# Last cross-attention of a four-layer Perceiver: the four query pieces of a tile spread over four steps, in banks 7, 5, 7 and 5

## The reference, cut to what matters

```python
def _L3_xattn_ref(image_embeds, latents, ln1_g, ln1_b, ln2_g, ln2_b, Wq, Wkv, Wo):
    x = layer_norm(image_embeds, ln1_g, ln1_b)          # (64, 257, 128)
    l = layer_norm(latents, ln2_g, ln2_b)               # (64, 32, 128)
    q = l @ Wq                                          # 16 heads of 64
    k, v = jnp.split(jnp.concatenate([x, l], axis=1) @ Wkv, 2, axis=-1)
    q, k, v = (to_heads(q), to_heads(k), to_heads(v))
    w = jax.nn.softmax(jnp.einsum('bhqd,bhkd->bhqk', q * scale, k * scale))
    out = jnp.einsum('bhqk,bhkd->bhqd', w, v)
    return out.transpose(0, 2, 1, 3).reshape(B, S_lat, INNER) @ Wo
x = x + _L3_xattn_ref(ctx_1024, _layernorm(x, axis=-1), ...)
```

## Time and profile before

| | us |
|---|---|
| median of 3 runs | 2186.41 (2182.8 to 2187.88) |
| profiled execution | 2167.64 |
| its span, first to last instruction | 2165.7 |
| mean granted TensorE clock | 0.916 |

### The profile page before, as it was taken

The page is one execution under the profiler, slowest core; times in us unless marked ns, Lnnn a source line. Parts: engine busy times, 40 slices in busy tenths (PEclk is TensorE's granted clock), DMA queues, the critical chain, the costliest instruction groups (busy, mean ns, idle before and its releaser), DMA issues. The chain is left out here.

```text
span 2165.7 us, 50175 instructions
## 1 busy us (share of the span) xinstructions
PE 1808.7 (84%) x20226; PEld 1196.8 (55%) x20226; DVE 1478.9 (68%) x3575; ACT 1013.0 (47%) x2544; POOL 731.6 (34%) x951
## 2 busy tenths in 40 slices
PE   6678999899978789986677799999999987756596
PEld 4324557556645556643556566777677652234386
DVE  6799995688875665557870477665666479987723
ACT  5535664566644722243412356666666422215243
POOL 2244554455541514214431311000000056533543
PEclk9778999999999999998779999999999998867688
DMA  8000000100026100080034201000000000021187
GB/s 343 1 1 0 1 0 1 75 5 5 5 80 277 42 2 1 1 331 2 2 116 128 65 25 37 13 20 20 21 20 1 1 1 10 19 101 71 32 296 239
DMA packets 57670, 130.63 MB, mean 60 GB/s; under 512 B 13961, under 2 KB 36188, under 8 KB 51808
## 3 DMA queue, kind: packets, MB, share of 16 engines
q1 hardware_dynamic: 54144, 121.32, 15.6%
q0 software_dynamic: 3296, 6.12, 0.8%
HBM read 107.97 MB, written 20.12 MB: 59 GB/s over the span
## 5 line engine op out<-in xcount | busy, mean ns | idle before, releaser
L319 POOL TENSOR_TENSOR arena<-arena 128x4 f32<-128x4 f32 (+2 forms) x97 | 113.9, 1176 | 772.9 <-DVE arena L263 336.4
L3293 ACT ACTIVATE arena<-PS,arena 128x289 f32<-128x289 f32 x256 | 127.4, 509 | 107.7 <-DVE arena L3401 107.7
L1870 POOL TENSOR_TENSOR arena<-arena 128x128 f32<-128x128 f32 x384 | 141.2, 409 | 42.8 <-PE PS L1733 20.0
L3401 DVE TENSOR_REDUCE arena<-PS 128x2 f32<-128x578 f32 x128 | 94.0, 755 | 76.3 <-PE PS L3181 76.3
L3181 PE MATMUL PS<-arena 128*128 128x289 f32 x512 | 135.5, 408 | 2.1 <-DVE arena L3395 0.9
L1806 DVE RECIPROCAL arena<-PS 128x128 f32<-128x128 f32 x96 | 91.5, 954 | 48.2 <-PE PS L1771 48.2
L1256 POOL TENSOR_TENSOR arena<-arena 128x512 f32<-128x512 f32 x64 | 84.0, 1313 | 109.9 <-DVE arena L1401 109.9
L1837 ACT COPY arena<-PS 32x128 f32<-32x128 f32 x384 | 99.5, 259 | 44.7 <-PE PS L1747 39.7
L3181 PEld LDWEIGHTS PS<-arena 128*128 128x128 f32 x512 | 92.2, 190 | 24.1 <-issue 2.2
L366 PE MATMUL PS<-arena 128*128 128x512 f32 x176 | 92.5, 658 | 12.4 <-DVEq L4199 11.7
L1852 ACT ACTIVATE arena<-arena 128x512 f32<-128x512 f32 x96 | 60.6, 631 | 65.7 <-DVE arena L1799 63.4
(11 more groups left out here) (419 smaller groups left out, 4774.2 us busy)
## 6 DMA issues: line engine op xcount, KB each, us to landing
arena<-in_ctx SPq DMA_DIRECT2D x32, 1091.0 KB, 10.2
arena<-in_f_w SPq DMA_DIRECT2D x39, 514.0 KB, 5.0
arena<-in_ctx SPq DMA_DIRECT2D x16, 834.0 KB, 14.7
lists<-arena SPq DMA_DIRECT2D x8, 1040.0 KB, 10.8
arena<-in_f_w SPq DMA_DIRECT2D x32, 256.0 KB, 3.1
arena<-in_ctx SPq DMA_DIRECT2D x16, 512.0 KB, 3.7
arena<-in_mid SPq DMA_DIRECT2D x1, 3796.5 KB, 11.9
arena<-in_late SPq DMA_DIRECT2D x1, 3204.0 KB, 10.3
```

Source lines behind the costliest of these rows:

```text
L319: e.tensor_tensor(x, x, half.broadcast_to(list(x.shape)), ALU.pow).then_inc(*T.done("norm_root", tag))
L1870: k = e.tensor_tensor(dst[:, b], spread(src[:, b, :], [P, HG, S], 1), spread(self.g.C["headmask"], [P, HG, S], 2), ALU.mult)
L3293: e.activation(self.weights(n, k, 0, UL), PS[:, k, 0:UL], ACT.Exp, bias=self.st[:, h, k:k + 1], accum_out=self.st[:, h, 4 + k:5 + k]).then ...
L3401: e.tensor_reduce(self.st[:, n % 2, 2 * k:2 * k + 2], PS[:, 2 * k:2 * k + 2, 0:UL], AXX, ALU.max, negate=True).then_inc(*T.done("k3_least" ...
```

## The change

The four pieces for tile i + 1 were made in tile i: piece 0 in step j=0 behind the key turn (bank 4), pieces 1 and 2 in step j=1 (banks 5 and 4), piece 3 in step j=2 (bank 4). Now one piece is made in each step. Step j=0 makes piece 0 in bank 7, ahead of the key turn; step j=1 piece 3 in bank 5; step j=2 piece 2 in bank 7. Piece 1 is made a tile earlier, in step j=3, in bank 5, for tile i + 2. As no tile lies in front of tile 1 for this, its piece 1 is made in step n=1, in bank 4. The same moves are made in TensorE's and in ScalarE's order. Which data is computed, and by which instructions, stays the same.

```diff
@@ def pe
             if i + 1 < NT and j == 0:
+                queries(i + 1, 0, 7)
                 key_turn(i + 1)
-                queries(i + 1, 0, 4)
             if n < NB and n % 2:
                 turn_thirds(n // 2)
+            if n == 1:
+                queries(1, 1, 4)
             if i + 1 < NT and j == 1:
-                queries(i + 1, 1, 5)
-                queries(i + 1, 2, 4)
+                queries(i + 1, 3, 5)
             if i + 1 < NT and j == 2:
-                queries(i + 1, 3, 4)
+                queries(i + 1, 2, 7)
             if i and j == 2:
                 project(i - 1)
             if i < NQ - 1 and j == 3:
                 cols_pe(e, T, g, "x3_lat", g.XN, free, (5,), qs=(i + 1,))
+            if i + 2 < NT and j == 3:
+                queries(i + 2, 1, 5)
```

## The result

| | before | changed |
|---|---|---|
| median of 19 runs, us | 2186.41 (2179.29 to 2195.17) | 2175.58 (2172.64 to 2182.93) |
| ratio, 95% interval | | 0.9957 (0.9946 to 0.9968) |
| span of the profiled execution, us | 2165.7 | 2173.2 |
| a steady tile, us | 30.495 | 29.484 |
| the stage in the profiled execution, us | 505.47 | 496.61 |

What follows compares the result with a forecast made beforehand. TensorE's stalls, read from start to start, set the tile. Eleven steady tiles at -1.0, first tiles +0.6 and first two steps +0.5 sum to -9.9 us: median 2176.5, own range 2173 to 2181 (2171.5 to 2184 against rivals).

Steps and rivals of the forecast that it cites:

- step j=0, bank 7: Steady tiles, step j=0: piece 0 in bank 7 ahead of the key turn ends the wait for ScalarE's copies, -0.58 us.
- steps j=1 and j=3: Steady tiles: one piece in bank 5 without wait in j=1, -1.34 us; the added piece in j=3, +0.89 us.
- tile 0, columns, seen at the turn of step 5: Tile 0, step j=3: new piece waits for the columns' copy out of bank 5; what follows is late by +1.29 us.
- tile 1, at the turn of step 9: Tile 1, step j=3: piece waits for ScalarE's columns copy; scores +2.29 us later, which VectorE hands all on.
- tile 2, at the turn of step 13: Tile 2, step j=3: scores +1.94 us later by the columns' copy, step j=0 gives back bubbles, so +1.00 us.
- first two steps: Stage start: two pieces start about 0.9 us later and run a little more at full clock, +0.5 us (-0.6 to +3.5).
- Rival A: Steady tiles: only the recorded idle returns, 0.48 us a tile; sum -2.6 us, median 2183.8 us; chance 0.13.
- rival C: Later stages take back the gain, so nothing moves beyond noise; near 2185 us; chance 0.03.
- VectorE and the covers at nothing: Steady tiles: VectorE's longer step j=3 and the j=3 piece's copy, with cover 1.4 us, were costed at 0.
- The added wait: Tiles 0 to 2, step j=3: piece behind the latent columns in bank 5 waits for their copy; scores +1.94, +2.29, +1.94 us.
- Rival B: New pauses at the columns and turns make the clock fall; five falls cost 17.5 us, giving 2194.0 us; chance 0.04.
- signs of being wrong: A 30.0 us tile; steady TensorE waits for banks 5, 7 or VectorE; second clock fall, 1257 to 1345; more time behind stage.

Runs made afterwards that it cites:

- bank alone: Kernel before with piece 0 of step j=0 in bank 7 instead of bank 4, still behind the key turn; tile 29.93 us, stage 498.65 us.
- the columns' experiment: Changed kernel with the latent columns of tiles 0, 1 and 2 turned in step j=2 into bank 4; ratio to before 0.992, stage 492.69 us.
- piece 0 put back: Changed kernel with piece 0 again in bank 4 behind the key turn; tile 30.05 us, stage 503.51 us.
- the four copies: Changed kernel with four extra ScalarE copies of bank 5 into unused buffers ahead of the step j=3 piece's copy; tile 29.95 us.
- both repairs: Changed kernel with latent columns in step j=2 in bank 4 and tile 1's piece 1 in bank 5; ratio to before 0.9925, stage 492.26 us.
- first banks: Changed kernel with tile 1's pieces 1 and 3 in step n=1 in their old banks, 5 and 4; stage 495.22 us.
- one pause filled: Changed kernel with four idle matmuls between scores and turn in step n=1; stage 496.42 us.
- both pauses: Changed kernel with columns and first-banks diffs, plus idle matmuls in both pauses of step n=1; ratio to before 0.9942, stage 489.54, then 490.25 us.

## Why the prediction was right, step by step

| term, us | forecast | shown |
|---|---|---|
| step j=0, bank 7 | -0.58 | -0.57 (tile 29.93, bank alone) |
| steps j=1 and j=3 | -1.34 + 0.89 | -0.44 (tile 30.05) |
| a steady tile | -1.0 | -1.011 |
| tile 0, columns, seen at the turn of step 5 | +1.29 | +1.32 |
| tile 1, at the turn of step 9 | +2.29 | +2.30 |
| tile 2, at the turn of step 13 | +1.00 | +1.02 |
| first two steps | +0.5 (-0.6 to +3.5) | +1.65; +0.53 in a second pair |
| stage | -9.9 | -8.86 and -9.99 |
| median | -9.9 | -10.8; by the ratio -9.4 (-11.8 to -7.0) |
| profiled execution | -9.9 (2157.7) | +7.6 (2175.2) |

The three rows of the first tiles come from the start of a row less the stage's start, in both traces, less what had piled up before. At the turn of step 5 that is 52.09 against 49.12, +2.97, of which 1.65 stood already; at step 9 it is +3.93, after the 1.34 saved in step 5; at step 13 +3.61.

- **What bounds.** Right. In the earlier trace rows TensorE is busy 29.52 of 30 at a granted clock of 1.00 and no other engine over 19.82, so time could come only from TensorE, and its starts were the thing to read: the recorded idle was 0.48 a tile and the gain 1.01. Rival A, which let only the idle come back, is out: a tile is 29.48, not 30.0. So is rival C: the interval of the ratio ends at 0.9968, and the gain lies in the stage.
- **VectorE and the covers at nothing.** Right. TensorE records no idle before a turn or a piece in the steady tiles, and the cover of the copy in step j=3 measured 1.5.
- **The added wait.** Right in place, and in size to 0.03 in each tile; the recorded pauses were 0.78, 1.14 and 0.78 where about 0.9, 1.3 and 0.9 were forecast. It cost 3.5 us by the columns' experiment, more than any other cost of the change that could be avoided, and nothing forces it: the columns can stand a step earlier, in the bank that the change has freed.
- **The first two steps.** The term that was mis-sized. Its +0.5 was the author's estimate, and no run shows it by itself; the two pairs showed +1.65 and +0.53. The estimate starts from TensorE's pause of 2.51 for VectorE and the granted clock of 0.51 behind it. VectorE's order was left alone, and the pause came out at 4.45. Behind the turn, piece 1 now waits in bank 4 for the thirds' copy (0.68 idle). The prediction had two effects: the piece starts about 0.9 later (shown: 24.50 against 23.47 after the stage's start, 1.03), and then runs a little more at the full clock (the reverse: 16 records took 3.51 to the scores against 2.89). The later start is mostly the wait on the thirds' copy, which the old banks remove. The other 0.62 is the half clock, which the prediction let end where it had ended before. It lasted longer: in the changed kernel all of these ten microseconds are at 0.50, where before it was some seven:

```profile
1251.00:1261.00 10.00, 6.75 (x28) 5.56 (x28) 9.00 (x39) 3.72 (x11) 3.79 (x6) 0.50 0.08 25
```

What counts for the scores is when it ends: 25.8 after the stage's start before, 27.9 in the changed kernel. Its length went with the pause before the turn of step 1 in all executions but one. With pauses of 2.51 to 3.22 (both executions of before, the bank alone, piece 0 put back) it was about seven microseconds, in all four executions; with pauses of 4.20 to 4.67 about ten in five (both of the changed kernel, the columns' repair, the four copies, both repairs) and seven in one (first banks, after 4.60). But its beginning moves too: in the second execution of before and with piece 0 put back, seven microseconds began later and ended at 28.0 all the same. So the longer pause that the change makes is a likely part of the 0.62; no run sets it apart from the moment of the fall, and the split stays open.

- **Rival B, a fall of the clock at the columns.** Not seen: pauses of 0.78, 1.14 and 0.78, some 32 us apart, left the clock at 1.00 (1262 to 1350). Nor did it fall in the steady tiles: before, with two small pauses in each (0.30 and 0.18), the granted clock was 1.00 over 1500 to 1530, and with pieces in banks 7, 5, 7 and 5, without these pauses, it is 1.00 from 1350 to 1700.

The sum was 1.0 too large for the first pair and right for the second. The second is luck in part: there the half clock of the kernel before happened to reach into the scores, 0.6 later than in the first. That the median came out within 0.9 of 2176.5 is closer than the interval of the gain (7.0 to 11.8) can tell. The 2157.7 for the profiled execution missed by 17.5, of which 1.0 is the stage; 2.0 arose ahead of the stage and 14.4 behind it. So one of its signs of being wrong did appear, more time behind the stage; but in the third batch, where both kernels ran on one chip, they take 441.7 and 441.8 there, so it is not of the change. The steady part of the stage repeats to a few hundredths and its first steps to about one microsecond, so the difference of two stages is good to about a microsecond, while the spans around them are not.

## What to carry to other kernels

Read a bound engine's stalls from start to start, not from its recorded idle: each of these waits cost about 0.2 to 0.3 us more than the profile calls idle (0.30 and 0.18 recorded, 0.58 and 0.45 paid). Where the piece waited for the copy of what TensorE had just written into its bank, another bank was enough (a tile of 29.93 for 30.495) and the order could stay. So try the bank first. And look through the whole loop for whoever else uses the new bank in the same step, in the first iterations too.

## What the runs showed of the hardware that was not expected

**Outside the stage, executions differ by more than the change is worth.** The stretch behind the stage, which is the same code in every kernel here, was either 429 to 432 us or 440 to 446 us long:

| executions | us behind the stage |
|---|---|
| profiled execution of before | 429.1 |
| first batch (piece 0 in bank 7; piece 0 put back; columns; one pause filled) | 429.3, 429.9, 430.4, 431.7 |
| profiled execution of the changed kernel | 443.5 |
| second batch (first banks; four copies; both repairs; both pauses) | 445.6, 444.7, 440.2, 445.7 |
| third batch (before; changed; both pauses) | 441.7, 441.8, 444.8 |

All kernels of a batch lie together, and so do the medians of the kernel before beside them: 2174.42 in the first batch, 2187.34 and 2185.91 in the others. So it goes with the batch, perhaps with the chip. Most of the difference arises at one instruction, a reciprocal of VectorE in a later layer. These are its rows in the two executions of the kernel before, 291.96 and 302.94 behind the stage:

```profile
2028.54 0.96 DVE L1806 RECIPROCAL arena<-PS 128x128 f32<-128x128 f32 x1 [1.21 <-PE PS L1771]
```

```profile
2046.15 0.96 DVE L1806 RECIPROCAL arena<-PS 128x128 f32<-128x128 f32 x1 [8.86 <-remote]
```

VectorE stood 1.2 to 1.3 before it in all five executions with the short stretch, and 8.8 to 10.4 in all eight with the long one. The profile names none of the core's engines as the releaser of the long wait (`remote`); its cause stays open. The start of the stage moved too, from 1231.1 to 1248.1. A comparison of two spans from different batches would have called this change slower.

**The clock fell behind three short pauses as well as behind a long one.** It fell, to 0.51, with one pause of 2.51. In the second execution of the same kernel the turn behind a pause of 2.58 still ran at a granted clock of 1.00, and it fell, to 0.50, only in the next pause:

```profile
1256.62 1.04 PE L3195 MATMUL PS<-arena 128*128 128x128 f32 x6
1259.16 1.11 PE L3204 MATMUL PS<-arena 128*128 128x128 f32 x4 [1.49 <-ACT arena L3310]
```

With the long pause filled it fell, to 0.50, behind 1.18, 1.49 and 0.80 within six microseconds, in which TensorE still ran. With pauses of 0.76 and 0.62, and of 1.24 and 0.63 in the second execution of that kernel, it stayed at 1.00.
